# Row maxima from the difference of two key halves, scores in three PSUM banks, and the attention output scaled on GpSimd

## The reference

```python
    q, k = (_rope(q), _rope(k))
    sim = jnp.einsum('bhid,bhjd->bhij', q, k) * SCALE
    attn = jax.nn.softmax(sim, axis=-1)
    out = jnp.einsum('bhij,bhjd->bhid', attn, v)
    out = out.transpose(0, 2, 1, 3).reshape(b, n, HEADS * DIM_HEAD)
    return out @ Wout + bout
```

## Time and profile before

| | us |
|---|---|
| median of 3 runs | 1557.63 (1556.99 to 1558.35) |
| the profiled execution | 1557.27 |
| its span in the trace | 1555.5 |
| busy PE / DVE / POOL / ACT | 1424.9 / 1222.0 / 977.8 / 778.3 |
| mean granted clock of PE | 0.986 |

### The profile page before, as it was taken

How to read it: one execution, slowest core, us unless ns; L and a number is a source line. 1 busy time by engine, 2 the same in 40 slices (tenths; PEclk the granted TensorE clock), 3 DMA queues, 4 the chain that set the end, 5 groups by cost and what they waited for, 6 DMA issues and landing times.

```text
span 1555.5 us, 25971 instructions
## 1 busy us (share of the span) xinstructions
PE 1424.9 (92%) x7289; PEld 546.8 (35%) x7289; DVE 1222.0 (79%) x1297; ACT 778.3 (50%) x1512; POOL 977.8 (63%) x501
## 2 busy tenths in 40 slices
PE   3689999999999999999999999999999999998886
PEld 1224333333333333333333333333333333333323
DVE  7787888788788878878788888878887887888744
ACT  3244554545454545555455454545545554544464
POOL 4388766658475665838476574848566584757731
PEclk9799999999999999999999999999999999999999
DMA  5312131221303121120313122031312204031002
GB/s 158 73 26 60 25 76 26 50 54 26 83 14 75 34 57 38 44 65 14 75 34 74 22 54 54 14 79 30 75 21 54 54 20 89 14 75 33 3 15 68
DMA packets 70209, 76.00 MB, mean 49 GB/s; under 512 B 27204, under 2 KB 36936, under 8 KB 69928
## 3 DMA queue, kind: packets, MB, share of 16 engines
q1 hardware_dynamic: 68736, 74.69, 21.4%
q10 hardware_dynamic: 1448, 1.00, 0.3%
HBM read 22.56 MB, written 2.36 MB: 16 GB/s over the span
## 4 chain that ended last, share of the span: by engine, by line
PE 56%; DVE 13%; issue 13%; POOL 7%; DMA 5%; ACT 3%; SPq 2%; DVEq 0%; ACTq 0%; POOLq 0%
PE O L388 18%; PE S L376 10%; PE S L377 8%; PE M L397 8%; DVE MX L603 5%; PE TILE L312 5%; DVE SUM L613 4%; DMA QK<-STAGE 4%; POOL SA L676 3%; PE TILE L322 2%; POOL STAGE L663 2%; ACT PF L515 2%; SPq L708 1%; PE TILE L306 1%; PE TILE L330 1%
## 5 line engine op out<-in xcount | busy, mean ns | idle before, releaser
L676 POOL TENSOR_TENSOR SA<-PF 128x1024 f32<-128x1024 f32 x256 | 616.5, 2424 | 372.5 <-DVE SUM L610 279.9
L515 ACT ACTIVATE PF<-S 128x512 f32<-128x512 f32 x1024 | 547.8, 599 | 564.9 <-PE S L377 564.1
L603 DVE TENSOR_REDUCE MX<-M 128x1 f32<-128x1024 f32 x504 | 614.5, 1219 | 229.3 <-PE M L397 229.1
L388 PE MATMUL O<-PF,V 128*64 128x512 f32 x2048 | 497.4, 607 | 0.0
L376 PE MATMUL S<-QK 128*128 128x512 f16 x1024 | 393.1, 384 | 0.0
L377 PE MATMUL S<-QK 128*128 128x512 f16 x1024 | 390.1, 381 | 0.0
L397 PE MATMUL M<-QK 64*128 64x512 f16 x1008 | 221.9, 437 | 65.9 <-DVE MX L603 47.7
L613 DVE TENSOR_TENSOR SUM<-SUM,SA 128x1024 f32<-128x1024 f32 x128 | 248.3, 1939 | 3.6 <-POOL SA L676 3.4
L397 PEld LDWEIGHTS M<-QK 64*128 64x128 f16 x1008 | 72.6, 140 | 370.8 <-DVE MX L603 247.9
L388 PEld LDWEIGHTS O<-PF,V 128*64 128x64 f32 x2048 | 124.5, 136 | 206.4 <-issue 149.8
L376 PEld LDWEIGHTS S<-QK 128*128 128x128 f16 x1024 | 99.9, 98 | 165.3 <-issue 64.2
(11 more groups left out here) (96 smaller groups left out, 749.0 us busy)
## 6 DMA issues: line engine op xcount, KB each, us to landing
QK<-STAGE SPq DMA_DIRECT2D x128, 256.0 KB, 3.9
QK<-STAGE SPq DMA_DIRECT2D x128, 128.0 KB, 3.1
RB<-den SPq DMA_DIRECT2D x128, 128.0 KB, 3.0
X<-in_L_attn_queries SPq DMA_DIRECT2D x4, 512.0 KB, 12.8
RT<-DS SPq DMA_DIRECT2D x128, 2.0 KB, 1.7
out<-X SPq DMA_DIRECT2D x8, 256.0 KB, 2.3
WRAW<-in_L_attn_Wkv SPq DMA_DIRECT2D x1, 1024.0 KB, 8.7
ROPE<-in_rope SPq DMA_DIRECT2D x1, 1024.0 KB, 12.0
```

Source lines behind the costliest of these rows:

```text
L388: mm = e.matmul(O[DH * z:DH * z + DH, :], V[:, h, kt * DH:(kt + 1) * DH], PF[:, t % SLOTS, z * HALF:(z + 1) * HALF], start=(kt == 0), stop ...
L515: e.activation(PF[:, t % SLOTS, z * HALF:(z + 1) * HALF], S[:, t % 2, z * HALF:(z + 1) * HALF], ACT.Exp, scale=EXP_SCALE).then_inc(exped, 1)
L603: e.tensor_reduce(MX[:, place % 2, q:q + 1], bank, AX, ALU.max).then_inc(max_read, 1)
L676: e.tensor_tensor(SA[:, (t // 2) % 2, :], PF[:, t % SLOTS, :], PF[:, t % SLOTS + 1, :], ALU.add).then_inc(two_summed, 1)
```

## The change

- A unit makes q (k1 - k2) in the bank MD and q k2 in one of two banks MR, with k1 and k2 the first and second 512 keys. The difference of the keys, KD, is a subtraction in f16 on POOL (`pool_keys_less`) and two more DMAs per head. ACT takes Relu of MD into LEFT, and DVE adds MR and LEFT and takes the maximum in one `tensor_tensor_reduce` over 512 columns.
- The scores have three banks in place of four, and other waits.
- OS is multiplied by RB on POOL (`norm`) at steps 13 and 26, the last one still on DVE.
- `act_copy_out` stands behind the Exps of its step.
- k is projected ahead of q. Tiles, and in the last iteration DOWN_AT, have other places.
- V1, B1R and U1 lie in SA, and the feed-forward part at the end uses other names for the same eight banks.

Cut to what matters (renamed index uses of `"qk"` to `ORDER`, the new semaphores, the prologue's order and the names of banks in the last part are left out):

```diff
-HAND = 4 * 16
+HAND = 6 * 16
...
-QK_TILES = [(w, c, t) for w in "qk" for c in range(2) for t in ("rot", "pass")]
+ORDER = "kq"
+QK_TILES = [(w, c, t) for w in ORDER for c in range(2) for t in ("rot", "pass")]
...
-QK_AT = (1, 3, 5, 7, 9, 11, 13, 15)
-V_AT = {8: (1, 0), 10: (1, 1), 22: (0, 0), 24: (0, 1)}
+QK_AT = (1, 3, 4, 7, 8, 10, 11, 13)
+KD_AT = 9
+V_AT = {14: (1, 0), 16: (1, 1), 22: (0, 0), 24: (0, 1)}
...
-NORM_AT = {16: 1, 26: 0}
+NORM_AT = {13: 1, 26: 0}
...
-        S = pb("S", [P, 2, N], F32)
-        M = pb("M", [P, N], F32)
+        S = pb("S", [P, 3, HALF], F32)
+        MD = pb("MD", [P, 512], F32)
+        MR = [pb(f"MR{n}", [P, 512], F32) for n in range(2)]
...
+        def bank_of(t, z):
+
+            return ((0, 1), (2, 0))[t % 2][z]
+
         def pe_scores(e, it, t):
...
             for z in range(2):
                 rows = slice(z * HALF, (z + 1) * HALF)
-                wait(e, exped, 2 * n + z - 3)
-                e.matmul(S[:, t % 2, rows], KHL[:, h, keys], QHH[:, h, rows], start=True, stop=False)
-                e.matmul(S[:, t % 2, rows], KMH[:, h, keys], QML[:, h, rows],
+                wait(e, exped, 2 * n + z - (0, 3)[t % 2 != z])
+                e.matmul(S[:, bank_of(t, z), :], KHL[:, h, keys], QHH[:, h, rows], start=True, stop=False)
+                e.matmul(S[:, bank_of(t, z), :], KMH[:, h, keys], QML[:, h, rows],
                          start=False, stop=True).then_inc(scored, 1)
...
+        def pe_unit(e, u, place, q, side):
+
+            wait(e, left_over, u)
+            wait(e, max_read, u - 1)
+            e.matmul(MD[:, :], QHH[0:DH, place, q:N:KT], KD[:, place, :], start=True, stop=True)
+            e.matmul(MR[side][:, :], QHH[DH:P, place, q:N:KT], KMH[DH:P, place, 512:N],
+                     start=True, stop=True).then_inc(unit_made, 1)
...
-            e.wait_ge(max_read, it.step(u))
-            pe_unit(e, it.step(u), place, q, M[:, :])
+            pe_unit(e, it.step(u), place, q, u % 2)
...
+        def act_left(e, u, side):
+
+            e.wait_ge(unit_made, u + 1)
+            wait(e, max_read, u - 1)
+            e.activation(LEFT[:, side, :], MD[:, :], ACT.Relu).then_inc(left_over, 1)
+
         def act_step(e, it, t):
...
-            if kt == 2 and (not it.first or h > 0):
-                act_copy_out(e, it.i * GH + h - 1, (h - 1) % GH)
+            more = not (it.last and t + LEAD >= STEPS)
+            if t % 2 == 0 and more:
+                act_left(e, it.step(t + LEAD), t % 2)
             for z in range(2):
...
+            if kt == 2 and (not it.first or h > 0):
+                act_copy_out(e, it.i * GH + h - 1, (h - 1) % GH)
             act_tiles(e, it, t)
+            if t % 2 == 1 and more:
+                act_left(e, it.step(t + LEAD), t % 2)
...
-        def dve_max(e, u, head, place, q, bank):
-
-            e.wait_ge(unit_made, u + 1)
+        def dve_max(e, u, head, place, q, side):
+
             if q == 0:
                 wait(e, max_found, head - 1)
-            e.tensor_reduce(MX[:, place % 2, q:q + 1], bank, AX, ALU.max).then_inc(max_read, 1)
+            e.wait_ge(left_over, u + 1)
+            e.sem_inc(max_begun, 1)
+            e.tensor_tensor_reduce(LEFT[:, side, :], MR[side][:, :], LEFT[:, side, :], 1.0, LOWEST, ALU.add, ALU.max,
+                                   MX[:, place % 2, q:q + 1]).then_inc(max_read, 1)
...
+        def pool_keys_less(e, g):
+
+            e.wait_ge(rot_hi, g * 4 + 2)
+            e.wait_ge(pass_hi, g * 4 + 2)
+            keys = HIGH["k"]
+            e.tensor_tensor(KDS[:, :, :], keys[:, :, 0:512], keys[:, :, 512:N], ALU.subtract).then_inc(keys_less, 4)
...
                 pool_sum(e, back % STEPS, it.i * (STEPS // 2) + back // 2, 3 * head + (-1, 0, 1, 1)[part])
+            if t in NORM_AT and not (it.first and NORM_AT[t]):
+                norm(e, it.pair(NORM_AT[t]), NORM_AT[t])
...
                 sp.dma_start(QK[top, h, 0:3:2, :], STAGE[rows, 1:3, t, :]).then_inc(handed[h], 16)
+                sp.dma_start(KD[top, h, :], KDS[rows, t, :]).then_inc(handed[h], 16)
                 sp.dma_start(QK[low, h, 0:4, :], STAGE[rows, 0:4, t, :]).then_inc(handed[h], 16)
...
                 if h == 0:
                     sp.wait_ge(rot_lo, (it.i + 1) * 4 + 4)
                     sp.wait_ge(pass_lo, (it.i + 1) * 4 + 4)
+                    sp.wait_ge(keys_less, (it.i + 1) * 4 + 4)
```

More of the change, by code:

```diff
@@ L27 @@
 EPS = 1e-5
-HAND = 4 * 16
+LOWEST = -3.0e38
+HAND = 6 * 16
 PV_LAG = 4
@@ L53 @@
 TURN_X_AT = (4, 7, 9, 11, 13, 15)
-DOWN_AT = (12, 14, 16, 18, 21, 23)
+DOWN_AT = (12, 18, 21, 22, 23, 24)
 HAND_ORDER = [("qk", 3), ("max", 1), ("sums", 1), ("inverse", 1), ("spread", 1), ("max", 2), ("qk", 0),
@@ L142, in build @@
         QML = QK[:, :, 3, :]
+        KD = sb("KD", [DH, GH, 512], F16)
+        KDS = sb("KDS", [P, 2, 512], F16)
         V = sb("V", [P, GH, KT * DH], F32)
@@ L152, in build @@
         SUM = sb("SUM", [P, 2, N], F32)
+        V1 = SA[0:3 * RANK, 0, 0:FF]
+        B1R = SA[0:FF // P, 1, 0:P]
+        U1 = SA[:, 1, FF:FF + RANK]
         ONES = sb("ONES", [P, 32], F32)
@@ L158, in build @@
         OS = sb("OS", [P, 2, 2, HALF], F32)
+        LEFT = sb("LEFT", [P, 2, 512], F32)
         MX = sb("MX", [P, 2, KT], F32)
@@ L171, in build @@
         QT = QK[:, 3, :, :].rearrange("p a b -> p (a b)").bitcast(F32)
-        S = pb("S", [P, 2, N], F32)
-        M = pb("M", [P, N], F32)
+        S = pb("S", [P, 3, HALF], F32)
+        MD = pb("MD", [P, 512], F32)
+        MR = [pb(f"MR{n}", [P, 512], F32) for n in range(2)]
         O = pb("O", [P, HALF], F32)
         T = pb("TILE", [P, 512], F32)
-        HB = [S[:, side, z * 512:(z + 1) * 512] for side in range(2) for z in range(2)]
-        OB = [O[:, :], M[:, 0:512]]
-        TB = [T[:, :], M[:, 512:1024]]
+        HB = [S[:, 0, :], S[:, 1, :], S[:, 2, :], MR[0][:, :]]
+        OB = [O[:, :], MR[1][:, :]]
+        TB = [T[:, :], MD[:, :]]
         x_in = [sem(f"x_in{b}") for b in range(B)]
@@ L191, in build @@
         pass_hi, pass_lo, v_made = sem("pass_hi"), sem("pass_lo"), sem("v_made")
-        added = sem("added")
+        added, keys_less = sem("added"), sem("keys_less")
         handed = [sem(f"handed{h}") for h in range(GH)]
-        unit_made, max_read, max_found, max_row = (sem(n) for n in ("unit_made", "max_read", "max_found", "max_row"))
+        unit_made, left_over, max_begun, max_read, max_found, max_row = (sem(n) for n in ("unit_made", "left_over", "max_begun", "max_read", "max_found", "max_row"))
         scored, exped, pv_done, o_copied = sem("scored"), sem("exped"), sem("pv_done"), sem("o_copied")
@@ L219, in freed @@
                 if t == "rot":
-                    return rot_read, g * 4 + "qk".index(w) * 2 + c + 1
+                    return rot_read, g * 4 + ORDER.index(w) * 2 + c + 1
                 if t == "pass":
-                    return pass_lo, g * 4 + "qk".index(w) * 2 + c + 1
+                    return pass_lo, g * 4 + ORDER.index(w) * 2 + c + 1
                 return v_made, (it.i + 1 - c) * 4 + 2 * c + t + 1
@@ L429, in act_tile @@
                 e.wait_ge(tile_made, made)
-                if w == "q" and c == 0:
+                if w == ORDER[0] and c == 0:
                     for h in range(GH):
@@ L445, in act_rot @@
             w, c, _ = args
-            nth = "qk".index(w) * 2 + c
+            nth = ORDER.index(w) * 2 + c
             e.wait_ge(rot_sum, g * 4 + nth + 1)
@@ L514, in act_step @@
                     wait(e, two_summed, (it.i * GH + h - 1) * (KT // 2) + kt // 2 + 1)
-                e.activation(PF[:, t % SLOTS, z * HALF:(z + 1) * HALF], S[:, t % 2, z * HALF:(z + 1) * HALF], ACT.Exp,
+                e.activation(PF[:, t % SLOTS, z * HALF:(z + 1) * HALF], S[:, bank_of(t, z), :], ACT.Exp,
                              scale=EXP_SCALE).then_inc(exped, 1)
+            if kt == 2 and (not it.first or h > 0):
+                act_copy_out(e, it.i * GH + h - 1, (h - 1) % GH)
             act_tiles(e, it, t)
+            if t % 2 == 1 and more:
+                act_left(e, it.step(t + LEAD), t % 2)
         def dve_tile(e, kind, args, made, g, bank):
@@ L640, in dve_step @@
                 dve_sum(e, it.i * GH + h - 1, (h - 1) % GH, SUM_AT[kt])
-            if t in NORM_AT and not (it.first and NORM_AT[t]):
-                dve_norm(e, it.pair(NORM_AT[t]), NORM_AT[t])
             if not (it.last and u >= STEPS):
-                dve_max(e, it.step(u), it.i * GH + u // KT, (u // KT) % GH, u % KT, M[:, :])
+                dve_max(e, it.step(u), it.i * GH + u // KT, (u // KT) % GH, u % KT, u % 2)
         def rot_add(e, args, g):
             w, c, _ = args
-            nth = g * 4 + "qk".index(w) * 2 + c
+            nth = g * 4 + ORDER.index(w) * 2 + c
             e.wait_ge(rot_read, nth + 1)
@@ L685, in pool_step @@
                     rot_add(e, args, it.i + 1)
+            if t == KD_AT and not it.last:
+                pool_keys_less(e, it.i + 1)
```

(17 more changed lines are left out.)

9 lines of the change are left out of this document (3 added, 6 removed).

## The result

| | before | changed |
|---|---|---|
| median, us | 1557.99 (1556.99 to 1561.87, 4 runs) | 1860.99 (1855.16 to 1865.42, 4 runs) |
| profiled span, us | 1555.5 | 1857.3 |
| mean granted clock of PE | 0.986 | 0.963 |

The ratio is 1.194 (95% interval 1.190 to 1.198): slower by 303 us. 1866 us had been forecast.

What follows compares the result with a forecast made beforehand. PE, busy 92% of the span, was taken as the bound. To 1557.3 us came 16 x (23.7-4.6) = 305, less 2 for the ends, plus 6 for the start: 1866 us, range 1795 to 1935, forecast case 77%.

Steps and rivals of the forecast that it cites:

- Holes given back (-4.6 per iteration): PE's seven holes per steady iteration, most ending on DVE's reduction L603, would be given back whole: -4.6 us.
- The wait (+23.7): In odd steps half z=1 waits for the Exp of half z=0 just before: PE stalls 23.7 us per iteration.
- the bare latency: Least PE stall per odd step, from score matmul through Exp to PE's restart, ACT's queue not counted: 1.06 us.
- the nine pairs: Step pairs 4, 6, 8, 16, 20, 22, 24, 28, 30, without copy-out: stalls of 10.0 us in all.
- The copy-out's place: Copy-out behind the even Exps, 1.20 us of ACT: stalls of 2.37 us each in pairs 2, 18, 26.
- Pair 0: Steps 0 and 1 of an iteration: ACT free at 2.14 us, so PE stalls 1.17 us.
- Clock: Rival: PE's clock falls to 1.2 GHz in a quarter of the iterations, adding 340 us: 2206 us, 4%.
- First and last iteration: Only 2 us off the 16 iterations' sum, for no copy-out at the first step 2 and missing units at the end.
- Tile of step 11 (+0.3): In pair 10, the tile after the pass tile also waits for DVE's read of that one: +0.3 us.
- Earlier tiles, POOL's product: nothing: Earlier tile places with two more DMAs per head, and the product moved to POOL, would cost PE nothing.
- The other rivals: Wait doesn't hold PE: 1490 us, 4%; only the bare latency: 1761, 8%; lateness spreads, 0.5 per pair: 1994, 7%.
- Start (+6): Twelve units in a row before the loop, slowed by the single difference bank, and two more issues: +6 us.

Runs made afterwards that it cites:

- copy_ahead: The changed kernel with the copy-out ACTIVATEs ahead of the Relu and Exps of their step, over-long wait kept: 1792.6 us, ratio to before 1.150.
- short_act_loop: holes_closed without ACT waits that others imply (pv_done, max_read, and two_summed in odd steps): 1600.2 us, ratio to before 1.027.
- after_short_act: The changed kernel, over-long wait kept, without the ACT waits that others imply: 1835.4 us.
- holes_closed: The changed kernel with odd-step half z=1 waiting for exped >= 2n-1, copy-out ahead of Relu, q, k, v tiles at their former steps: 1601.2 us, ratio 1.029.
- early_tiles: short_act_loop with most q and k tiles earlier, two v tiles at steps 16 and 18, output tiles at 17 and 21: 1546.8 us, ratio to before 0.993.
- product_on_dve: holes_closed with the product of OS and RB back on DVE at steps 16 and 26: 1603.5 us.

## Why the prediction was right

The forecast case came: 1861 measured against 1866, with the mechanism that had been named. That the two lie within 5 us is in part luck: three terms were off by more than that, and they cancel.

- *Holes given back (-4.6 per iteration).* Right. No line of PE waits for the reduction in steady state. Its waits for the Relu (9.1 us in all, 13 times) all lie before 70 us of the span, in the units ahead of the loop and the first steps.
- *The wait (+23.7).* Right as a mechanism: undoing it alone takes 290 us away, adding it alone to the kernel before brings 222. As a size it was 1.7 too high, 28 us over 16 iterations. The term that was mis-sized is the bare latency: 1.06 forecast, 0.86 measured in pair 8, and 8.3 for 10.0 in the nine pairs that it rules. The Exp starts 0.42 after the last matmul of its half (748.39 to 748.81), not 0.57 as in the earlier trace rows, and PE restarts 0.05 after the Exp's end, not 0.10.
- *The copy-out's place.* Right: 2.26 to 2.47 against 2.37. Its price by copy_ahead is 68 us, of which the shorter holes are about half (2.1 us per iteration) and the clock that it pulls down the rest.
- *Pair 0.* Wrong, 1.94 against 1.17. The prediction had no term for ACT's late start at the head of the loop (2.5 to 2.7 us, "issue" in the waits above). short_act_loop and after_short_act show that it goes when ACT's loop has fewer instructions.
- *Clock.* It had been a rival at 4%, with a quarter of the time at the lower level. It came in a small form, 1.4 or 3.1 us per iteration, 2.2 in the mean, which happens to fill the gap that the shorter latency left. So the sum of a steady iteration is better than its terms: 85.0 + 21.9 + 2.2 = 109.1 against 85.0 + 23.7 = 108.6.
- *First and last iteration.* The forecast took 19.1 us for each of the 16 and 2 off. The trace has 19.5 for each of the 14 in the middle, but 13.2 in the first (98.0 to 111.3) and 12.0 in the last (90.1 to 102.1, first to last score matmul): 11 us less than forecast for the two. Their waits for an Exp sum to 19.4 and 20.0; what else differs in them was not followed up.
- *Tile of step 11 (+0.3).* In the changed kernel nothing; it is 1.74 once the wait is gone. *Earlier tiles, POOL's product: nothing.* True for this kernel. But holes_closed and early_tiles show the tiles' places to be worth much as soon as PE is not held elsewhere, and product_on_dve shows the product's place on POOL to be worth 0.7 us per iteration there.
- *The other rivals.* PE did wait, ACT's order did cost, and the lateness did not spread: in the steady iterations looked at PE waits for nothing but the Exps.
- *Start (+6).* The first Exp of the kernel came at 62.3 us against 57.9, so 4.3.

## What to carry to other kernels

When banks are reused in an uneven pattern, work out for each write which reader last had the bank, and wait for that one: a count that is too high by two made a wait for work issued an instant before, and cost 290 of this kernel's 1861 us. A stage's wait is priced by when its releaser ends, with all that stands ahead of that on its own engine, and not by the number of waits. And undo a loss one step at a time: behind the wait lay holes for the tile bank, the hand-over and the copy-out that it had covered, and the version better than before (by 0.7%) had all of them moved.

## What was not expected of the hardware

- With ACT idle, an Exp can start 0.42 us after the start of the last matmul of its half, and in the earlier trace rows it took 0.57. It is not that more matmuls follow: in the changed kernel the Exp starts after 0.41 with a tile's matmuls right behind. What makes the difference is open.

```profile
720.74 0.38 PE L388 MATMUL S<-QK 128*128 128x512 f16 x1
720.96 0.82 PE L319 MATMUL TILE<-XT,WQK 128*128 x3
...
721.15 0.60 ACT L532 ACTIVATE PF<-S 128x512 f32<-128x512 f32 x1 [0.70 <-PE S L388]
```

- ACT waited 2.5 to 2.7 us at the head of 13 loop passes with 80 packets of instructions in the trace, and not at all with 14 packets, after 80 waits (32 for pv_done, 32 for max_read, 16 for two_summed) had been taken out of its loop. The loop before had 12.
- The clock falls to its lower level behind some holes of 2.0 to 2.5 us and not behind others of the same length, and it stays there for about 3 us. It can also fall behind a shorter one: in the changed kernel behind a hole of 1.94 us (1045.16 to 1047.31) the granted clock was 0.66, while behind the same hole at 720.51 it was 1.00. By the Trainium skill (TensorE: Matmul & The Clock Gate, section "What's actually happening") the chip's check of TensorE's activity is not tied to when the program starts; that the same hole ends either way agrees with it. The windows behind the two holes of 1.94 us:

```profile
1048.00:1053.00 5.00, 5.00 (x16) 1.26 (x15) 1.95 (x5) 1.26 (x3) 1.04 (x1) 0.66 0.00 0
721.00:725.00 4.00, 4.00 (x20) 1.34 (x20) 1.96 (x6) 1.76 (x3) 0.00 (x0) 1.00 0.00 0
```
